# Turning TensorE's loops inside a step of a recurrence, and spreading its gate products over four steps

## What is computed

```
gi = x_t @ W_ih + b_ih                  # input gates, for every step t
gh = h @ W_hh + b_hh                    # 512 x 1536 weights, h is (4, 512)
r = sigmoid(i_r + h_r)
z = sigmoid(i_z + h_z)
n = tanh(i_n + r * h_n)
h = (1 - z) * n + z * h                 # the state that the next step needs
```

## Time and profile before

| | us |
|---|---|
| median of three runs | 2145.55 |
| the profiled execution | 2142.75 |
| its span in the trace | 2141.0 |
| TensorE busy | 2076.2 (97%) |
| DVE busy | 1352.5 (63%) |
| ACT busy | 1240.6 (58%) |
| POOL busy | 630.1 (29%) |
| matmuls of the steps, line 1219, 65536 records | 1448.9 |
| matmuls of the gate pieces, lines 1247 and 1258, 5376 records | 193.9 |

### The profile page before, as it was taken

One profiled execution on the slowest core, in us unless ns is written; L12 is line 12 of the kernel. 1 busy time (PEld: TensorE's weight loads), 2 busy tenths in 40 slices (PEclk: granted clock), 3 DMA queues, 4 the chain that ended last, 5 costly groups with the idle time before them and its releaser, 6 DMA issues.

```text
span 2141.0 us, 178103 instructions
## 1 busy us (share of the span) xinstructions
PE 2076.2 (97%) x76072; PEld 1620.8 (76%) x76072; DVE 1352.5 (63%) x6162; ACT 1240.6 (58%) x5995; POOL 630.1 (29%) x1011
## 2 busy tenths in 40 slices
PE   8999999999999999999999999999999999999997
PEld 2222222222499999999999999999999999998887
DVE  3344445444367777777777777777777777776666
ACT  3444544543266666666666666666666666666665
POOL 0355545444112222222222222222222222222222
PEclk9999999999999999999999999999999999999999
DMA  6000000011222121212222122222221212210001
GB/s 256 1 1 1 1 1 1 1 50 41 52 53 54 50 57 49 56 49 52 71 52 55 50 53 51 55 66 57 52 56 47 56 50 64 62 31 7 5 7 20
DMA packets 218076, 95.99 MB, mean 45 GB/s; under 512 B 170216, under 2 KB 213480, under 8 KB 217320
## 3 DMA queue, kind: packets, MB, share of 16 engines
q1 hardware_dynamic: 217032, 92.00, 16.5%
q10 hardware_dynamic: 928, 2.65, 0.3%
HBM read 26.30 MB, written 12.58 MB: 18 GB/s over the span
## 4 chain that ended last, share of the span: by engine, by line
PE 67%; DVE 5%; issue 1%; DMA 0%; ACT 0%; SPq 0%; DVEq 0%
PE ps L1219 61%; PE ps L1247 4%; DVE arena L1044 4%; PE ps L1258 2%; DVE arena L1062 1%; DMA arena<-arena 0%; DVE arena L940 0%; DVE arena L1050 0%; DVE arena L1057 0%; DVE arena L943 0%; ACT arena L1186 0%; SPq L969 0%; DVE arena L1134 0%; DVE seq L1139 0%; ACT arena L1175 0%
## 5 line engine op out<-in xcount | busy, mean ns | idle before, releaser
L1219 PE MATMUL ps<-whh,arena 128*4 128x128 f32 (+1 forms) x65536 | 1448.9, 246 | 35.2 <-DVE arena L1062 27.0
L1219 PEld LDWEIGHTS ps<-whh,arena 128*4 128x4 f32 x65536 | 1350.8, 87 | 92.4 <-DVE arena L1062 63.3
L1044 DVE STREAM_TRANSPOSE arena<-ps 128x64 f32<-128x64 f32 x2048 | 445.8, 284 | 264.7 <-PE ps L1219 246.5
L1175 ACT ACTIVATE arena<-arena 128x8 f32<-128x8 f32 x1024 | 216.3, 211 | 561.1 <-DVE arena L1044 500.6
L441 DVE TENSOR_REDUCE top<-ps 128x2 f32<-128x1024 f32 x128 | 150.8, 1220 | 254.5 <-PE ps L699 254.5
L1150 ACT ACTIVATE ps<-arena 128x128 f32<-128x128 f32 x1026 | 288.8, 282 | 0.5 <-PEq L207 0.4
L1062 DVE TENSOR_TENSOR_SCAN arena<-arena 128x24 f32<-128x24 f32 x1024 | 193.3, 189 | 145.2 <-ACT arena L1186 145.2
L1050 DVE STREAM_TRANSPOSE arena<-ps 128x64 f32<-128x64 f32 x1024 | 256.8, 251 | 8.2 <-PE ps L1219 3.0
L347 ACT ACTIVATE arena<-ps 128x1024 f32<-128x1024 f32 x128 | 124.1, 1021 | 212.4 <-PE ps L775 212.3
L596 PE MATMUL ps<-arena 128*32 128x512 f32 x2048 | 243.9, 598 | 2.7 <-ACT arena L369 2.7
L940 POOL TENSOR_TENSOR arena<-tap,arena 128x128 f32<-128x128 f32 x252 | 101.9, 415 | 439.5 <-DVE seq L1075 439.5
(11 more groups left out here) (97 smaller groups left out, 1218.0 us busy)
## 6 DMA issues: line engine op xcount, KB each, us to landing
arena<-arena SPq DMA_DIRECT2D x216, 114.0 KB, 2.2
arena<-arena SPq DMA_DIRECT2D x112, 128.0 KB
arena<-seq SPq DMA_DIRECT2D x224, 55.0 KB
arena<-gi_d SPq DMA_DIRECT2D x248, 32.0 KB
gi_d<-arena SPq DMA_DIRECT2D x96, 57.0 KB
out<-seq SPq DMA_DIRECT2D x14, 256.0 KB
seq<-in_x SPq DMA_DIRECT2D x3, 1024.0 KB, 15.8
whh<-in_w_hh SPq DMA_DIRECT2D x1, 3072.0 KB, 20.9
```

The costliest lines, as they stand in the source:

```text
L1044: e.transpose(trn[:, h, q].rearrange("p (i c s) -> p c i s", c=2, s=2)[:, :, :, 0], bank[RN[h]][:, 64 * q:64 * q + 64].rearrange("p (c i) ...
L1175: e.activation(r_d0[:, h].rearrange("p (i s) -> p i s", s=2)[:, :, 1], trn[:, h, 0, 0:2 * NH].rearrange("p (i s) -> p i s", s=2)[:, :, 0], ...
L1219: last = e.matmul(bank[dst[h]][32 * G:32 * G + B, 0:n], hv, wv[:, k, gates, G, 64 * h:64 * h + 64], start=False, stop=k2 == 1 and k == C - ...
```

## The change

`step` is cut in two. `begin(t, u)` holds its first two groups (rn of both halves from h0) with their waits, and `end(t, u)` the rest. Before the first loop `begin(0, 0)` is issued. In a loop's body each step is `end` of this step, a gate piece, `begin` of the next step, so that both loops turn between the second and the third group of a step. After the last step one more `begin` is issued, whose products nothing reads.

The gate pieces of a body are cut by chunk: k = 0 and 1 of rz behind the first step, k = 2 behind the second, k = 3 of rz and k = 0 of n behind the third, and k = 1 of n behind the fourth.

```diff
+                def begin(t, u):
+                    half = (count(2 * t + 1), count(2 * t + 2))
                     e.wait_ge(st["s_h"], half[0])
                     e.wait_ge(st["s_seed_rn"], half[0])
-                    products(RN, rn, 0, 0)
+                    products(u, RN, rn, 0, 0)
                     e.wait_ge(st["s_seed_rn"], half[1])
-                    products(RN, rn, 1, 0)
+                    products(u, RN, rn, 1, 0)
+
+                def end(t, u):
+                    half = (count(2 * t + 1), count(2 * t + 2))
                     e.wait_ge(st["s_h"], half[1])
...
                 e.wait_ge(st["s_clear"], N_CLEAR)
+                begin(0, 0)
                 with e.Fori(0, BODIES) as it:
                     for v in range(4):
-                        step(it * 4 + v, v % 2)
-                        if v < 2:
-                            part_rz(v, it)
+                        end(it * 4 + v, v % 2)
+                        if v == 0:
+                            part_rz((0, 1), it)
+                        elif v == 1:
+                            part_rz((2,), it)
                         elif v == 2:
-                            part_n(it)
+                            part_rz((3,), it)
+                            part_n(0, it)
+                        else:
+                            part_n(1, it)
+                        begin(it * 4 + v + 1, (v + 1) % 2)
                 with e.Fori(2 * BODIES, T // 2) as it:
                     for v in range(2):
-                        step(it * 2 + v, v)
+                        end(it * 2 + v, v)
+                        begin(it * 2 + v + 1, 1 - v)
```

More of the change, by code:

```diff
@@ L1208, in _ @@
                 wv = whh[:].rearrange("p c (q G n) -> p c q G n", q=3, G=NG)
[L1210 to L1223, removed]
+                rn, z = slice(0, 3, 2), slice(1, 2)
@@ new lines, in products @@
+                def products(u, dst, gates, h, k2):
+                    n = len(range(3)[gates]) * 64
+                    for k in (2 * k2, 2 * k2 + 1):
+                        hv = h_of(u, k // 2).rearrange("p (b c) -> p b c", c=2)[:, :, k % 2]
+                        for G in range(NG):
+                            last = e.matmul(bank[dst[h]][32 * G:32 * G + B, 0:n], hv, wv[:, k, gates, G, 64 * h:64 * h + 64],
+                                            start=False, stop=k2 == 1 and k == C - 1, skip_group_check=True)
+                    return last
@@ L1224, in step, with count @@
+                def count(v):
+                    return v if isinstance(v, int) else e.snap(v)
+                def begin(t, u):
+                    half = (count(2 * t + 1), count(2 * t + 2))
                     e.wait_ge(st["s_h"], half[0])
                     e.wait_ge(st["s_seed_rn"], half[0])
-                    products(RN, rn, 0, 0)
+                    products(u, RN, rn, 0, 0)
                     e.wait_ge(st["s_seed_rn"], half[1])
-                    products(RN, rn, 1, 0)
+                    products(u, RN, rn, 1, 0)
@@ L1229, in step @@
+                def end(t, u):
+                    half = (count(2 * t + 1), count(2 * t + 2))
                     e.wait_ge(st["s_h"], half[1])
-                    products(RN, rn, 0, 1).then_inc(st["s_rn"], 1)
+                    products(u, RN, rn, 0, 1).then_inc(st["s_rn"], 1)
                     e.wait_ge(st["s_seed_z"], half[0])
-                    products(RZ, z, 0, 0)
-                    products(RZ, z, 0, 1).then_inc(st["s_z"], 1)
-                    products(RN, rn, 1, 1).then_inc(st["s_rn"], 1)
+                    products(u, RZ, z, 0, 0)
+                    products(u, RZ, z, 0, 1).then_inc(st["s_z"], 1)
+                    products(u, RN, rn, 1, 1).then_inc(st["s_rn"], 1)
@@ L1235, in step, with part_rz @@
                     e.wait_ge(st["s_seed_z"], half[1])
[L1236 to L1241, removed]
+                    products(u, RZ, z, 1, 0)
+                    products(u, RZ, z, 1, 1).then_inc(st["s_z"], 1)
+                def part_rz(ks, q):
+                    if ks[0] == 0:
                         e.wait_ge(st["s_ataken"], e.snap(q + 1))
-                    e.wait_ge(s_apair[v], e.snap(q * 32 + 32))
-                    for k in (2 * v, 2 * v + 1):
+                    if ks[0] != 3:
+                        e.wait_ge(s_apair[ks[0] // 2], e.snap(q * 32 + 32))
+                    for k in ks:
@@ L1248, in part_rz @@
                                             start=k == 0, stop=k == C - 1)
[L1249 to L1260, removed]
+                    if ks[-1] % 2:
+                        last.then_inc(st["s_rzpart"], 1)
@@ new lines, in part_n @@
+                def part_n(k, q):
+                    if k == 0:
+                        e.wait_ge(st["s_nseed"], e.snap(q + 1))
+                        e.wait_ge(st["s_npair"], e.snap(q * 48 + 48))
+                    for g in range(NG):
+                        rows = slice(32 * g, 32 * g + 32)
+                        last = e.matmul(bank[FN][rows, 0:CW], n_fixed[:, k, rows], n_moving[:, k, :],
+                                        start=False, stop=k == 1, skip_group_check=True)
+                    if k == 1:
+                        last.then_inc(st["s_npart"], 1)
```

## The result

The changed kernel takes 2133.90 us, median of 6 runs (2133.13 to 2136.42), against 2144.97 us for the kernel before in 6 runs. The ratio is 0.995 (0.9948 with one digit more), 95% interval 0.994 to 0.996: the medians differ by 11.1 us. The forecast was 2146 us with a range of 2137 to 2155, so the time lies under the range, even a little beyond the case "the turn is hidden" (2136 to 2140.5). The profiled execution took 2133.52 us with a span of 2131.7.

The account below looks back on a forecast made before the run. The state's 2.97 us round trip or TensorE's own work bounds each step. 112 x (0.07 - 0.085) + 32 x 0.07 = +0.5 us on 2145.55 gave 2146 us, range 2137 to 2155.

Parts of the forecast that it names:

- the turn is hidden: Rival: at the new place the turn costs 0 to 0.03 us, whole chunk gain stays, 2136 to 2140.5 us; chance 0.25.
- The round trip as a floor: Both loops: a step lasts the larger of the state's round trip, 2.97 us, and TensorE's own work.
- Part one: First loop: spreading gate chunks two, one, two, one saves 0.085 us a body, 9.5 us over 112 bodies.
- Part two: Loop turn behind the second rn group: sequencer loses x = 0.07 us a turn ahead of the third group.
- The lead is eight products in both: Sequencer runs eight products ahead of the array at two trace places, so 0.436 us ahead with 128-column products.
- 144 x - 9.5: Whole kernel: time difference in us, with x the cost of one turn at the new place, over 144 turns.
- One sign that the forecast had named: Changed kernel's chain: second and fourth step should show DVE's transposes and the scan.
- The rival with x over 0.10: Rival: waits hold the sequencer, so a turn costs 0.12 to 0.15 us, 2153 to 2157 us; chance 0.20.
- The Trainium skill's queue of 64: TensorE queue: counted in trace records, a lead of sixteen products and a turn cost of 0; weighed as a rival only.
- Part three: What else moves: second loop's 32 turns cost 2.2 us; SP's later waits, DVE, extra products and code fetch cost nothing.

Follow-up runs that it names:

- the version with one and a half chunks: Changed kernel with one rz and one n chunk each cut in two by columns, so every step has one and a half chunks: 0.9905, 2126.07 us.

## Why the prediction was wrong

**The round trip as a floor, 2.97 us: right.** Steps with one chunk measure 2.971 and 2.973 us in the changed kernel and steps with one and a half 2.972 and 2.973.

**Part one, the chunks, -0.085 us a body: right in size** (12.081 to 12.000, thus -0.081), but the forecast treated it as separate from the turn. It exists only with the turn moved; the chunks alone cost 6.4 us.

**Part two, the turn, x = 0.07 us: wrong. This is the step that failed**, in the sentence "The lead is eight products in both, so eight of 128 columns give 0.436 us". The duration of the turn was right up to its load: 0.472 us where 0.475 were taken (runs with the turn behind the third group and behind the fourth rn group). From there to the product it is 0.007 us in these runs and not 0.03, so 0.48 in all. The count was right too: 16 of the 32 matmul records of `begin` had not begun when the turn ran. What was wrong is to turn that count into time as if the running products were at their end. Both places from which I took the lead have 64-column products ahead of the last eight. There the sequencer's instruction ran with 12 loads and 16 matmul records left, as in the changed kernel, but only 0.003 to 0.004 us before the first of these matmuls began, so that their own time was all the lead. Four records of 64 columns begin every 0.055 us, four of 128 columns every 0.109. In the changed kernel the instruction ran just after four of them had begun, and 0.085 us passed before the next four did. So the lead is 0.085 + 4 x 0.109 = 0.52 us and the turn fits under it. Why the sequencer passes at just that moment isn't shown, and the count itself isn't fixed: 14 and 18 were left in 12 of 111 turns of the changed kernel's first loop, 16 and 20 with the chunks one, two, one, two. The run behind the fourth rn group, wide products behind narrow ones, gives the 0.44 of my formula; the change just doesn't stand there.

The product behind the turn stands at the same 0.876 us with and without a turn, so x is 0, and the forecast's formula, 144 x - 9.5, gives -9.5 us. The profiled executions say -9.2. In them rare long bodies cost less than before (mean over median 0.023 us instead of 0.034, 1.2 us in all), which the start and the second loop take back. The medians say -11.1: the profiled execution of the kernel before lay 2.2 us under its median, that of the changed kernel 0.4. The runs of one kernel scatter by 3.3 to 3.4 us, so this difference isn't explained further. One sign that the forecast had named failed as well: the chain of the changed kernel shows no transpose and no scan in the second and fourth step, though these steps do last the round trip.

**The margin.** I gave "x from 0 to 0.03" a chance of 0.25 and said that no row shows the lead at 128 columns. That was the weak place, and it should have weighed more than two agreeing rows of another kind. The rival with x over 0.10, where a wait holds the sequencer, is real but one group away: it came out when the turn stood behind a group that waits late, for h1.

**The Trainium skill's queue of 64** (TensorE: Matmul & The Clock Gate, Architectural detail: the array is 16× 32×32, not 1× 128×128) gave the right result, x = 0, by a lead that isn't there: 28 records had not begun at the turn (12 loads and 16 matmuls), and 36 in the run with the chunks one, two, one, two, not 64.

**Part three:** no gate piece waits for a DMA more than before (0.3 us on line 1255, 0.3 before on 1247), and the instruction queue of the earlier trace rows has 47 packets again. The second loop was forecast at +2.2 us and gave +0.3, for the same reason as the first.

## What to carry to other kernels

A hardware loop's turn is free where the array still has more queued work than the turn lasts (0.48 us here). Read that work as a time in the trace, from the turn's first instruction to the product due behind it, and not as a number of products: it was 0.22 us behind narrow products, 0.44 behind wide ones that follow narrow ones, and 0.52 to 0.57 behind wide ones that follow wide ones. Don't put the turn behind a group that waits late. Compare each step's own work with the round trip of its recurrence, and level the filler work so that every step stays just under it: two, two, two, none left 0.2 us a body, and one and a half everywhere took nearly all of it. Two edits that look separate may only pay together, so read what each does alone to the next wait.

## What I had not expected of the hardware

The same turn of the second loop, at the same place among the same instructions, costs nothing in the changed kernel and about 0.09 us in the version with one and a half chunks. There the sequencer's next own instruction behind the eight products after the turn runs 0.77 us after the turn's first, and 0.59 us after it in the first loop and in both loops of the changed kernel (medians). One turn of each, the version with one and a half chunks first (window 1993.2 to 1994.1 us), then the changed kernel (1996.8 to 1997.6 us); the first row is the turn's first instruction, the second the one behind the eight products:

```profile
L1289 PEldq ALU_OP  x1: 32/32/32, 1993.2 to 1993.2; - x1
L1238 PEldq ALU_OP  x1: 36/36/36, 1994.0 to 1994.0; - x1
...
L1287 PEldq ALU_OP  x1: 32/32/32, 1996.8 to 1996.8; - x1
L1238 PEldq ALU_OP  x1: 36/36/36, 1997.4 to 1997.4; - x1
```

The first transpose of the step starts 0.09 us later for it. Only the code ahead of the loop differs, by eight more matmul instructions and the waits and widths of the cut pieces. The code isn't fetched again: from 1926 to 2120 us neither instruction queue moved a packet in that version. Where the loop lies in instruction memory may matter in another way, but no run here tests it. The long turns behind the fourth rn group, where the loads stopped a second time, look like the same thing.
